# Moving keys times queries behind the 32-column products, and token numbers through memory, in an attention and mixture-of-experts kernel

## The reference

```
xn  = layernorm(x)
q,k = elu(two linear maps of xn) + 1, v = two linear maps of xn       # 16 heads of depth 8
S   = sum over rows l of k[l]^T q[l]      per batch and head (8 x 8)
out = (v @ S) / (sum(q * k) + 1e-6), then @ Wo + bo
attention = gamma * normalise(xn + out) + beta
gates  = softmax(xn @ wg.T), 64 experts, the best 8 per token, renormalised; at most 160 rows an expert
experts: h = rows @ w1.T; (x1 * silu(x2)) @ w2.T, scaled by the gate and added to the token's row
shared : the same feed-forward for every token
result = x + attention + shared + experts
```

## Time and profile before

| | us |
|---|---|
| median of 3 runs | 342.9 (342.28 to 344.78) |
| span of the profiled execution, first to last instruction | 340.5 |
| busy: PE / PEld / DVE / ACT / POOL | 331.0 / 311.1 / 275.8 / 205.6 / 240.9 |

### The profile page before, as it was taken

One profiled execution on the slowest core, in us unless ns is written; L12 is line 12 of the kernel. 1 busy time (PEld: TensorE's weight loads), 2 busy tenths in 40 slices (PEclk: granted clock), 3 DMA queues, 4 the chain that ended last, 5 costly groups with the idle time before them and its releaser, 6 DMA issues.

```text
span 340.5 us, 9358 instructions
## 1 busy us (share of the span) xinstructions
PE 331.0 (97%) x3099; PEld 311.1 (91%) x3099; DVE 275.8 (81%) x1136; ACT 205.6 (60%) x450; POOL 240.9 (71%) x243
## 2 busy tenths in 40 slices
PE   8899999999999999999999999999999999999995
PEld 8798899899899999999999999999999999999982
DVE  3799897997778778797989798988878897846585
ACT  3789934565556595757475947475677565674220
POOL 5687733667888878878877788888887877877400
PEclk9999999999999999999999999999999999999999
DMA  7999533699787878887878787878878878863699
GB/s 201 364 385 322 148 91 117 228 297 296 177 227 170 234 164 226 186 211 196 214 196 214 173 214 184 210 184 202 211 183 220 186 207 186 200 138 33 141 344 280
DMA packets 60112, 71.16 MB, mean 209 GB/s; under 512 B 14881, under 2 KB 47905, under 8 KB 60065
## 3 DMA queue, kind: packets, MB, share of 16 engines
q1 hardware_dynamic: 42592, 56.40, 52.1%
q0 software_dynamic: 15360, 13.12, 24.8%
q10 hardware_dynamic: 2112, 1.05, 1.0%
HBM read 54.72 MB, written 15.43 MB: 206 GB/s over the span
## 4 chain that ended last, share of the span: by engine, by line
PE 69%; ACT 9%; DMA 8%; issue 5%; DVE 4%; POOL 4%; SPq 0%; POOLq 0%; DVEq 0%; ACTq 0%
PE bank L1368 25%; PE bank L1378 10%; PE bank L1293 8%; PE bank L1302 4%; PE bank L1413 3%; PE bank L1387 3%; DMA ew<-acc 2%; PE bank L1419 2%; DMA acc<-ys,idx_g 2%; PE bank L1437 2%; DMA gath<-xng,idx_g 2%; ACT L541 2%; PE bank L1453 2%; POOL acc L507 2%; ACT L544 2%
## 5 line engine op out<-in xcount | busy, mean ns | idle before, releaser
L507 POOL DMA_INDIRECT acc<-ys,idx_g x64 | 103.4, 1616 | 25.8 <-issue 13.7
L1368 PE MATMUL bank<-xe,ew 128*128 128x160 f32 x768 | 116.6, 301 | 0.6 <-ACT xe L605 0.4
L1368 PEld LDWEIGHTS bank<-xe,ew 128*128 128x128 f32 x768 | 107.4, 190 | 2.3 <-ACT xe L605 1.3
L488 POOL DMA_INDIRECT gath<-xng,idx_g x80 | 80.9, 1011 | 33.3 <-issue 21.3
L569 ACT ACTIVATE si<-bank 128x480 f32<-128x480 f32 (+1 forms) x96 | 52.0, 542 | 58.9 <-PE bank L1368 29.8
L783 DVE TENSOR_TENSOR ac<-si,bank 128x480 f32<-128x480 f32 x64 | 41.6, 651 | 17.6 <-ACT si L569 15.1
L1378 PE MATMUL bank<-ew,ac 128*128 128x128 f32 x384 | 53.4, 275 | 0.0
L1378 PEld LDWEIGHTS bank<-ew,ac 128*128 128x128 f32 x384 | 49.5, 192 | 1.0 <-issue 0.2
L1293 PE MATMUL bank<-xT,shw 128*128 128x128 f32 x384 | 48.3, 276 | 0.0
L1293 PEld LDWEIGHTS bank<-xT,shw 128*128 128x128 f32 x384 | 46.2, 194 | 0.1
L611 ACT ACTIVATE ys<-bank,gath 128x128 f32<-128x128 f32 x64 | 23.5, 368 | 13.3 <-PE bank L1378 13.3
(11 more groups left out here) (172 smaller groups left out, 591.6 us busy)
## 6 DMA issues: line engine op xcount, KB each, us to landing
ew<-in_expert_w SPq DMA_DIRECT2D x64, 384.0 KB, 3.7
ew<-in_expert_w SPq DMA_DIRECT2D x64, 192.0 KB, 3.4
ew<-acc SPq DMA_DIRECT2D x8, 512.0 KB, 7.0
x_sb<-in_x SPq DMA_DIRECT2D x8, 256.0 KB, 6.4
xng<-xn SPq DMA_DIRECT2D x8, 256.0 KB, 4.6
acc<-zeros SPq DMA_DIRECT2D x4, 512.0 KB, 5.1
acc<-betas SPq DMA_DIRECT2D x4, 512.0 KB, 2.8
gath<-xng,idx_g POOLq DMA_INDIRECT x80, 3.8
```

What stands on the lines that cost most here:

```text
L488: pool.indirect_dma_start(out=gath[:, p, m, :], out_offset=None, in_=xng, in_offset=bass.IndirectOffsetOnAxis(ap=idx_g[:, g % 4, m:m + 1], ...
L507: pool.indirect_dma_start(out=acc[adds_to[g, m]], out_offset=bass.IndirectOffsetOnAxis(ap=idx, axis=0), in_=src, in_offset=None, compute_o ...
L1368: last = pe.matmul(h_view(n, half_ + 1, CAP)[:, c, :], ew[p][m][:, k * P:(k + 1) * P], xe[:, p, m, :], start=True, stop=True)
```

## The change

Three things change places or way. `values` and `keys_queries` go forward in PE's order, `keys_queries` to right behind `down_rest`, and `values_copy` on ScalarE goes ahead of `load_silu`. The token numbers of the remaining rows are stored to memory in one DMA (128 runs of 4 bytes) and read back in a second one as a row that goes to all 128 partitions. `rest_repeat` and `rest_turn` go away, and with them the use `same` of bank A.

```diff
-        a_uses += [('rest', g - 1), ('sum', g - 1)] * (g > 0) + [('same', g)] + [('table', g + 2)] * (g + 2 < NG)
+        a_uses += [('rest', g - 1), ('sum', g - 1)] * (g > 0) + [('table', g + 2)] * (g + 2 < NG)
...
+        rest_d = dram("rest_d", [NG, P])
...
+            def rest_store(g):
+                sp.wait_ge(v_ready, g + 1)
+                at_least(sp, rest_moved, 32 * g)
+                sp.dma_start(rest_d[g:g + 1, :].rearrange("o p -> p o"), v_rest[:, g:g + 1]).then_inc(rest_moved, 16)
+            def rest_load(g):
+                sp.wait_ge(rest_moved, 32 * g + 16)
+                at_least(sp, eq_ready, g - 1)
+                sp.dma_start(vrow[:, g % 2, :], rest_d[g, :].partition_broadcast(P)).then_inc(rest_moved, 16)
...
             for q in range(1, 3):
                 counts_in(q)
+            rest_store(0)
             sp.wait_ge(betas_set, 1)
             for k in range(0, 1024 * N_ACC, 1024):
                 sp.wait_ge(h1_full, up_at['e', 0, min(k // 1024, 2)] + 1)
                 fill(0, k)
+                if k == 0:
+                    rest_load(0)
...
                 up_weights(g + 1, 1)
+                rest_store(g + 1)
...
                 up_weights(g + 1, 3)
+                rest_load(g + 1)
...
                     exp_of(g + 1)
+                    values_copy(g + 1)
                     load_silu()
                 pair_copy(g)
                 silu(('e', g, 1))
                 if g > 0:
                     rest_copy(g - 1)
-                if attend:
-                    values_copy(g + 1)
...
-            def rest_repeat(g):
-                if g == 0:
-                    dve.wait_ge(ones_set, 1)
-                else:
-                    dve.wait_ge(a_full, a_at['same', g - 1] + 1)
-                dve.wait_ge(v_ready, g + 1)
-                dve.tensor_scalar(vrep[:, :], ones[:, :], v_rest[:, g:g + 1], None, ALU.mult).then_inc(vrep_ready, 1)
             def rest_same(g):
-                dve.wait_ge(a_full, a_at['same', g] + 1)
-                dve.tensor_scalar(eq[:, g % 2, :], A[:, 0:P], v_rest[:, g:g + 1], None, ALU.is_equal).then_inc(a_done, 1)
+                dve.wait_ge(rest_moved, 32 * (g + 1))
+                if g > 1:
+                    dve.wait_ge(a_full, a_at['sum', g - 2] + 1)
+                dve.tensor_scalar(eq[:, g % 2, :], vrow[:, g % 2, :], v_rest[:, g:g + 1], None, ALU.is_equal).then_inc(eq_ready, 1)
...
             def rest_sum(g):
                 pe.wait_ge(a_done, a_at['sum', g])
+                pe.wait_ge(eq_ready, g + 1)
...
-            def rest_turn(g):
-                pe.wait_ge(vrep_ready, g + 1)
-                pe.wait_ge(a_done, a_at['same', g])
-                pe.transpose(A[:, 0:P], vrep[:, :], ident).then_inc(a_full, 1)
...
                 if a < B:
                     queries_keys(a)
+                    values(a)
                 up(g, 1)
                 pair_rows(g)
                 if g > 0:
                     down_rest(g - 1)
                 if a < B:
-                    values(a)
+                    keys_queries(a)
                 down(g, 0)
                 up(g, 2)
                 if g > 0:
                     rest_sum(g - 1)
                 down(g, 1)
-                if a < B:
-                    keys_queries(a)
-                rest_turn(g)
```

More of the change, by code:

```diff
@@ L184, in block_kernel @@
         ys = sb("ys", [P, M + 2, D])
-        vrep, eq, dup_t = sb("vrep", [P, P]), sb("eq", [P, 2, P]), sb("dup_t", [P, P])
+        vrow, eq, dup_t = sb("vrow", [P, 2, P]), sb("eq", [P, 2, P]), sb("dup_t", [P, P])
         dup, first_, vr = sb("dup", [P, 1]), sb("first", [P, 1]), sb("vr", [P, 1])
@@ L235, in block_kernel @@
         xr_done, wr_step, wrest_done = sem("rest_rows_copied"), sem("wrest_step"), sem("wrest_done")
-        vrep_ready, dup_step, idxr_ready = sem("vrep_ready"), sem("dup_step"), sem("idx_rest_ready")
+        eq_ready, dup_step, idxr_ready = sem("eq_ready"), sem("dup_step"), sem("idx_rest_ready")
+        rest_moved = sem("rest_tokens_moved")
         eu_ready, f_ready, qk_ready, qks_step, rq_ready = (sem(n) for n in
@@ L920, in rest_gate @@
                 dve.tensor_reduce(wrest[:, g % 2:g % 2 + 1], wr_t[:, :], AX.X, ALU.add).then_inc(wrest_done, 1)
-            def rest_repeat(g):
-                if g == 0:
-                    dve.wait_ge(ones_set, 1)
-                else:
-                    dve.wait_ge(a_full, a_at['same', g - 1] + 1)
-                dve.wait_ge(v_ready, g + 1)
-                dve.tensor_scalar(vrep[:, :], ones[:, :], v_rest[:, g:g + 1], None, ALU.mult).then_inc(vrep_ready, 1)
             def rest_same(g):
-                dve.wait_ge(a_full, a_at['same', g] + 1)
-                dve.tensor_scalar(eq[:, g % 2, :], A[:, 0:P], v_rest[:, g:g + 1], None, ALU.is_equal).then_inc(a_done, 1)
+                dve.wait_ge(rest_moved, 32 * (g + 1))
+                if g > 1:
+                    dve.wait_ge(a_full, a_at['sum', g - 2] + 1)
+                dve.tensor_scalar(eq[:, g % 2, :], vrow[:, g % 2, :], v_rest[:, g:g + 1], None, ALU.is_equal).then_inc(eq_ready, 1)
             def rest_first(g):
-                dve.wait_ge(a_done, a_at['same', g] + 1)
+                dve.wait_ge(eq_ready, g + 1)
                 dve.scalar_tensor_tensor(dup_t[:, :], eq[:, g % 2, :], 1.0, earlier[:, :], ALU.mult, ALU.mult, accum_out=dup[:, 0:1]).then_inc(dup_step, 1)
@@ L1106, in _ @@
                 if g > 0:
-                    rest_repeat(g)
                     rest_gate(g)
```

## The result

The changed kernel takes 410.51 us (median of 4 runs, 408.2 to 427.64), the kernel before on the same chip 343.62 us. The ratio is 1.194, 95% interval 1.189 to 1.200: 67 us slower where 2 us faster was forecast. The profiled execution spans 408.3 us.

A forecast was written before the change was run, and what follows sets the result against it. POOL was taken to set the end: it gets 2.6 us from PE's 4.2, less 0.5 lost at the start, so 2.1 us; span 338.4 + 2.4 = 340.8 us. Range, 8 in 10: 338.6 to 343.8.

The forecast's parts named there:

- Part 4: Token numbers' way through memory: added packets cost the DMA engines 1.1 us a group, share 0.83 to 0.90; `rest_same` shouldn't wait.
- Part 1: PE, keys times queries moved and transpose dropped: a group gains 0.38 us, bounds 0.26 and 0.52.
- Part 2: Features `f` needed earlier on PE: 1.1 us lost in group 0, charged at nothing; elsewhere a wait of 0 to 0.1.
- Part 3: ScalarE's order, `values_copy` ahead of `pair_copy`: covered by 0.2 us in steady groups; groups 4, 8 and 12 gain 0.1.
- rival (c): PE's 4.2 us pass whole, POOL losing its waits and long instructions: 338.7 us, or 337.3 by the upper bound; chance 0.16.
- Rival (d): Added packets lengthen the landing of the remaining rows' scatter, slowing each POOL group; at 0.3 us, 344.5 or 346.1; chance 0.14.

The follow-up runs named there:

- the row in SBUF: The changed kernel, with the 128 values first gathered into one row of SBUF and stored to memory in one piece: 341.99 us, ratio 0.996 to the kernel before.
- the order alone: The kernel before with only the new order of values, keys times queries and values_copy; repeat and transpose stay: 341.67 us, ratio 0.996.
- group 0 spared: The kernel before with the new order alone in groups 1 to 15, group 0 keeping the old order: 341.33 us, ratio 0.995.

## Why the prediction was wrong

**Part 4 failed**, at one step: "No row shows runs of 4 bytes. Between nothing and twice the packet's time I take the packet's time." The bound was too narrow above. It priced packets by the time that each takes of an engine, 1.1 us of 16 engines a group. Measured, a dense store costs 3.9 us of the kernel's time, and packets of others take up to 6.9 us behind it, where none took 2 before. The same 128 packets at 64 bytes apart cost nothing that shows, so a price per packet was the wrong form, whatever its size. The rule of the Trainium skill that I weighed (DMA: Bandwidth & Descriptors, Specifications: under 512 bytes read-modify-write) pointed at the right instruction. Taken as a doubling of short packets it left no mark in any run: 4 bytes long and 64 or 512 bytes apart, or 64 bytes long and side by side, all measured 342.7 to 343.8 us. That overlapping read-modify-writes queue up would explain the doses; no run shows it.

**The rest of Part 4 held.** The load cost 0.5 us at the most likely (343.26 against 342.77, an interval around no change). The DMA share of a steady group was forecast to rise from 0.83 to 0.90. It was 0.85 with the row in SBUF, and 0.86 in the same place of the order alone, which adds no packet, so the added packets don't show in it. `rest_same` waited for `vrow` once, 2.3 us, and only in the disturbed stream of the changed kernel.

**Part 1 was right.** A group went from 16.30 to 15.93 us: 0.37, forecast 0.38. Without the transpose's 0.16 the forecast was 0.22, and the order alone gave 165.84 - 149.76 = 16.08, again 0.22. From first instruction to first instruction the group before took 166.00 - 149.68 = 16.32, which makes it 0.25 here and 0.39 above. (The recorded expectation of that run took 0.11 for the transpose and said 0.27.) Its timeline of PE, the first instruction of two groups running:

```profile
149.76 1.88 PE L1367 MATMUL bank<-xe,ew 128*128 128x160 f32 x12
...
165.84 0.93 PE L1367 MATMUL bank<-xe,ew 128*128 128x160 f32 x5
```

The pieces show where the change of width went. Keys times queries costs 161.94 - 161.70 = 0.24, not the 0.14 of its own pace. But the 24 ahead of it now take 161.70 - 161.02 = 0.68. In the kernel before they took 0.80, from here to the 159.64 of the earlier trace rows:

```profile
158.84 0.86 PE L1387 MATMUL bank<-ew,ac 128*32 128x128 f32 x24
```

So 0.24 - 0.12 = 0.12 net stands for the 0.14. The rest of the way back to full width, 0.10, is in the next down product (162.71 - 161.94 = 0.77 instead of 0.67), and `values` no longer pays it (159.08 - 158.65 = 0.43 instead of 0.53).

**Part 2 was right in its times and wrong in its charge.** PE waits 1.58 us for `f` in group 0, to 61.67 (forecast: `f` at 61.69), and in no other group. The weights of group 1 came late once, by 1.2 us with the row in SBUF and 1.3 with the order alone; forecast was up to 1.6. But "I charge it at nothing", because PE's surplus over POOL would hide it, doesn't fit the two timelines above: PE carried 1.34 us of it to group 15, and 1.35 us arrived at POOL's last scatter.

**Part 3 held in the steady groups and was too bright for groups 4, 8 and 12.** They were to gain 0.1 us each. In the order alone PE waits there for `pair_copy`, 0.23, 0.23 and 0.16 us, and nowhere else for it. Its timeline in group 4:

```profile
128.75 1.90 PE L1367 MATMUL bank<-xe,ew 128*128 128x160 f32 x12 [0.23 <-ACT xe L605]
```

From its first up product to that of the next group, group 4 took 137.42 - 120.77 = 16.65 us before and 137.75 - 121.04 = 16.71 here. With the transpose gone too, in the kernel with the row in SBUF, it took 139.56 - 122.81 = 16.75. So these groups lose about 0.1 where 0.1 was to be gained, a small term of the sum.

**What bounds the kernel** seems misread with it. POOL's 16.0 us a group against PE's 16.3 made me say that PE's gain passes only as far as POOL waits, 2.6 us in all. With group 0 spared 2.76 us passed to POOL, which is just what PE had gained by group 15, and POOL still waits 1.51 us for `ys` there, where I had expected nothing. That is the mechanism of rival (c): PE sets the pace. The rival asked that POOL's long instructions go as well, and they are gone: the longest scatter takes 1.81 us in both orders, 2.05 before. The change isn't shown to be the cause, for kernels with an unused load or a store 32 bytes apart have none over 1.83 either. Neither the forecast nor (c) had the step behind POOL, the landing of the last scatter, which took back what POOL had gained. The sum came out close all the same, 2.1 us forecast against 1.4 (0.5 to 2.3) without the dense writes and 1.3 (0.5 to 2.1) for the order alone, with group 0's loss and that landing in the place of POOL's limit. That closeness is luck.

**Rival (d)** had the direction and the mechanism nearly right, a landing lengthened by the added packets, and POOL behind it. Its size was 0.3 us. The median landing of a scatter rose by 1.5, from 3.5 to 5.0 us, and went up to 10.6, that of a gather rose by 4.6, and the rival looked only at the remaining rows' scatter: POOL waited 11.0 us for that and 60.7 for the others. Its premise, that added packets lengthen landings in proportion, is what the spread stores refute.

## What to carry to other kernels

A transfer whose elements are a few bytes each isn't priced by its bytes or packets: look at where the elements of the written side lie, and let neighbouring ones in memory be written by one piece (gather into a row of SBUF first) or spread them (from 16 bytes apart on, no cost showed here). A transfer that nobody waits for can still be the dearest of the kernel, so price it by what it does to landings of others, and read the GB/s slices and the landings next to the queue's share. Where no row shows the form of an operation, let the range say so on the dear side too: mine ended at twice the nearest row.

## What the runs showed of the hardware

- Sixteen stores of 512 bytes, as 128 dense values of 4 bytes, added 63 us to a kernel of 343. Of 127 such values, written by one DMA engine instead of 16, it was 131. The same values 16 bytes apart or more measured at most 1.2 us above the kernel before, and into one SBUF row nothing that shows.
- The DMA engines count as busy meanwhile: q1's share rose from 52.1% to 57.5% while 12 to 90 GB/s moved for 6 us of the group read above. A busy share isn't a rate.
- With PE idle for 44 us in 22 waits for gathers, the longest 4.9, the granted clock averaged 0.93 where it was full before, and 18.7 of the 67.8 us were PE's longer busy time.
- The way from 32 columns back to full width cost 0.2 us: in the timelines above 0.12 on the narrow instructions and 0.10 on the wide ones behind them.
- The last scatter took 3.6 to 7.0 us to land in kernels that differ little, so 2.8 us gained ahead of it didn't reach the end of the profiled execution.
